# Early scores from straight q and k copies, and the experts' bias as a second matmul in the last half, in a two-layer attention and experts kernel

## The reference, cut to what matters

```python
# layer 1 (a = 0 in the kernel, work "p1" ahead of it, "p2" behind it)
x = x + attn(layernorm(x))        # q, k, v by one 8x24 matrix per head; softmax(att * mask), mask = tril(k=-1)
# layer 2 (a = 1, work "p2" ahead of it, "p3" behind it)
q_in = k_in = rope(xn); v_in = xn # causal softmax attention, xn = layernorm(x)
x1  = layernorm(xn + attn_out) * ln1_w + ln1_b
gates = softmax(x1 @ gate_w.T + gate_b); top_idx = top_k(gates, 2)
expert_outputs = einsum("bsd,efd->bsef", x1, expert_w) + expert_b     # 8 experts
moe = sum over the two chosen experts of expert_outputs * top_gates
out = x + layernorm(x1 + moe) * ln2_w + ln2_b
```

## Time and profile before

| | us |
|---|---|
| median of 3 runs | 789.04 (788.24 to 795.55) |
| the profiled execution's own time | 789.42 |
| its span in the trace | 787.6 |
| PE busy | 681.1 (86%) |
| ACT busy | 648.1 (82%) |
| DVE busy | 395.9 (50%) |
| POOL busy | 322.9 (41%) |

### The profile page before, as it was taken

How to read it: one execution, slowest core, us unless ns; L and a number is a source line. 1 busy time by engine, 2 the same in 40 slices (tenths; PEclk the granted TensorE clock), 3 DMA queues, 4 the chain that set the end, 5 groups by cost and what they waited for, 6 DMA issues and landing times. The chain is left out here.

```text
span 787.6 us, 15418 instructions
## 1 busy us (share of the span) xinstructions
PE 681.1 (86%) x5568; PEld 259.9 (33%) x5568; DVE 395.9 (50%) x1062; ACT 648.1 (82%) x721; POOL 322.9 (41%) x635
## 2 busy tenths in 40 slices
PE   4798998988899989989897989989999789999853
PEld 2333333433234333233232333233333233233422
DVE  5355344456445453556244644574345765455573
ACT  1499997999899997999698889998889798888721
POOL 3162235323633434434553245532666314424334
PEclk9589998999999997999898999999999999999976
DMA  6848357535567432424455244423545451230100
GB/s 162 288 136 263 101 202 239 178 127 202 181 213 243 162 110 86 148 83 135 143 163 155 104 141 130 146 83 121 190 151 179 158 162 60 70 96 1 41 13 15
DMA packets 77142, 109.86 MB, mean 139 GB/s; under 512 B 13928, under 2 KB 28400, under 8 KB 77040
## 3 DMA queue, kind: packets, MB, share of 16 engines
q1 hardware_dynamic: 72944, 107.32, 42.8%
q10 hardware_dynamic: 4096, 1.33, 0.8%
HBM read 60.94 MB, written 47.68 MB: 138 GB/s over the span
## 5 line engine op out<-in xcount | busy, mean ns | idle before, releaser
L1504 ACT ACTIVATE probs<-scores,shift 128x1024 f32<-128x1024 f32 x576 | 601.4, 1124 | 80.2 <-PE scores L1309 73.7
L1580 POOL TENSOR_SCALAR_AFFINE_SELECT probs<-probs 128x256 f32<-128x256 f32 (+1 forms) x448 | 197.5, 458 | 379.8 <-ACT probs L1504 379.1
L1334 PE MATMUL acc<-probs,v 128*9 128x512 f32 (+3 forms) x3072 | 322.2, 508 | 10.7 <-ACT num L1429 9.5
L1309 PE MATMUL scores<-qs,ks 32*128 32x512 f32 (+3 forms) x1536 | 185.1, 434 | 41.0 <-ACT probs L1504 37.4
L1309 PEld LDWEIGHTS scores<-qs,ks 32*128 32x128 f32 x1536 | 83.1, 189 | 259.9 <-ACT probs L1504 175.0
L1334 PEld LDWEIGHTS acc<-probs,v 128*9 128x9 f32 x3072 | 59.1, 100 | 132.2 <-issue 72.9
L1627 DVE TENSOR_TENSOR prod<-side,G 128x512 f32<-128x512 f32 x48 | 33.1, 691 | 89.3 <-PE side L1275 79.3
L1275 PE MATMUL side<-we,x1T 128*128 128x512 f32 x100 | 58.6, 669 | 0.8 <-DVE x1T L1916 0.8
L1561 POOL TENSOR_TENSOR moe<-psum 128x256 f32<-128x256 f32 x32 | 24.4, 762 | 51.3 <-DVE x1b L1627 26.6
L1429 ACT ACTIVATE num<-acc 128x512 f32<-128x512 f32 x64 | 38.2, 596 | 5.3 <-PE acc L1334 5.2
L1536 POOL TENSOR_TENSOR rstd<-rstd,expo 128x4 f32<-128x4 f32 x32 | 33.4, 1044 | 2.7
(11 more groups left out here) (186 smaller groups left out, 602.4 us busy)
## 6 DMA issues: line engine op xcount, KB each, us to landing
ks<-k_dram SPq DMA_DIRECT2D x96, 256.0 KB, 4.1
q_dram<-part SPq DMA_DIRECT2D x64, 256.0 KB, 3.5
qs<-q_dram SPq DMA_DIRECT2D x64, 256.0 KB, 3.2
num_dram<-num SPq DMA_DIRECT2D x60, 256.0 KB, 3.3
k_dram<-part SPq DMA_DIRECT2D x30, 256.0 KB, 4.0
xrow<-in_x SPq DMA_DIRECT2D x16, 256.0 KB, 4.4
nat<-num_dram SPq DMA_DIRECT2D x15, 256.0 KB
rdenb<-rden_dram SPq DMA_DIRECT2D x15, 256.0 KB
```

Source lines behind the costliest of these rows:

```text
L1309: ins = pe.matmul(dst, ks[u][r, kt // TH, (kt % TH) * P:(kt % TH + 1) * P], qs[u][r, q0:q0 + w], start=True, stop=not shifted)
L1334: ins = pe.matmul(acc[h * VW:h * VW + VC, q0:q0 + w], v9[V_OF[k]][:, kt, :, HG * hg + h], src, start=(s == 0), stop=last, skip_group_check ...
L1504: act.activation(dst, src, ACT.Exp, bias=shift[:, column(st):column(st) + 1], scale=SCALE).then_inc(probs_raw, 1)
L1580: ins = pool.affine_select(out=blocks, in_=blocks, compare_op=ALU.is_ge, fill=0.0, base=a - 1, pattern=[[0, blocks.shape[1]], [1, P]], cha ...
```

## The change

**At the start.** The first two passes (`STRAIGHT = 2`) no longer read q and k back from DRAM: six DMAs on SP's queue and two on ACT's copy 32 partitions of `part` straight into `qs` and `ks` as soon as `q` and `k` of the first half are read. The stores to DRAM stay (the second half's passes and the third pass on read them). DVE makes the rows of the first half ahead of `pairs`, and its q terms ahead of `roots`. Four of the jobs (`k` and `v` of the second half, both `suffix`) are issued by PE behind the scores of sets 0, 0, 1 and 3 (`BEHIND`), with banks given by hand (`BEFORE_BANKS`), and a set waits only for the jobs in its own banks (`PAIR_FREE`). The loads of `earlier8`, `bars8`, `cos` and `sin` move from ACT's queue to SP's, behind the stores of the second half. The planner's clocks of DVE and SP begin at 5.0, and it puts no jobs at the first sets, so 230 of its places (all in the first half of the stream) move by a few points.

**In the tail.** `GT` and `bias` of the last half are gone. Each of its eight `e0`/`e1` jobs gets a second matmul into the same bank, a row of ones by the row `be_row` of four experts' biases, and POOL adds `x1` itself. `stats`, `root`, `centre`, `scale` and `store` of that half become two sets, A for tiles 4 and 5, B for 6 and 7. The planner of `AFTER` has other rules: `num` first, and a read by ACT counts only once its operands are there.

```diff
+BEFORE_BANKS = {("p1", 0, "xT", 0): 1, ("p0", 0, "pairs", 0): 0, ("p0", 0, "bound", 0): 2, ("p1", 0, "q", 0): 3, ("p1", 0, "k", 0): 0,
+                ("p1", 0, "xT", 1): 4, ("p1", 0, "q", 1): 5, ("p1", 0, "k", 1): 4}
+BEHIND = {("p1", 0, "k", 1): 0, ("p1", 0, "v", 1): 0, ("p1", 0, "suffix", 1): 1, ("p1", 0, "suffix", 0): 3}
...
-    clock = {"PE": 0.0, "ACT": 0.0, "DVE": 0.0, "POOL": 0.0, "SP": 0.0}
+    clock = {"PE": 0.0, "ACT": 0.0, "DVE": 5.0, "POOL": 0.0, "SP": 5.0}
...
-        room = True
+        room = g > max(BEHIND.values())
...
+PAIR_FREE = [max(n for n in range(N_BEFORE) if JOB_BANK[n] // 2 == i) + 1 for i in range(PAIRS)]
...
+        def q_straight(engine, gp, i):
+            src = part[0][32 * gp:32 * gp + 32, 0, i, :].bitcast(F32)
+            engine.dma_start(qs[gp][i::2, :].bitcast(F32), src.unsqueeze(1).broadcast_to([32, 2, HALF])).then_inc(qs_in[gp], 16)
+        def k_straight(engine, gp, i):
+            engine.dma_start(ks[gp][i::2, 0, :].bitcast(F32), part[0][32 * gp:32 * gp + 32, 1, :, :].bitcast(F32)).then_inc(qs_in[gp], 16)
...
             for x in BEFORE:
+                if x[:4] == ("p1", 0, "parts_out", 0):
+                    sp.wait_ge(side_free, done(("p1", 0, "q", 0)))
+                    for i in range(2):
+                        q_straight(sp, 0, i)
+                    sp.wait_ge(side_free, done(("p1", 0, "k", 0)))
+                    k_straight(sp, 0, 0)
+                    for i in range(2):
+                        q_straight(sp, 1, i)
+                    k_straight(sp, 1, 0)
                 if x[5]:
                     turn(*x[:4])
                 if x[:4] == ("p1", 0, "parts_out", 0):
-                    load(0)
-                    load(1)
+                    load(2)
+            for t, d in ((earlier8, earlier8_d), (bars8, bars8_d)):
+                sp.dma_start(t[:, :], bc(d)).then_inc(late_weights_in, 16)
+            for t, d in ((cos, cos_d), (sin, sin_d)):
+                sp.dma_start(t[:, :, :], d.rearrange("(t p) f -> p t f", p=P)).then_inc(late_weights_in, 16)
...
-                if g == 0:
-                    pe.wait_ge(side_free, N_SCORES)
-                elif last >= PAIRS:
+                for unit in UNITS_OF[g]:
+                    if unit < PAIRS:
+                        pe.wait_ge(side_free, PAIR_FREE[unit])
+                if last >= PAIRS:
                     pe.wait_ge(probs_raw, last - PAIRS + 1)
...
                 if (work, b, name, i) == ("p1", 0, "parts_out", 0):
+                    act.wait_ge(side_free, done(("p1", 0, "k", 0)))
+                    for gp in range(STRAIGHT):
+                        k_straight(act, gp, 1)
                     k_out(act, 0, b, i)
...
-                        signal(pe.matmul(out[:, :], x1T[i // TH][:, i % TH, :], we[:, first:first + HALF], start=True, stop=True), last)
+                        alone = (1, b, i // TH) == LAST_HALF
+                        ins = pe.matmul(out[:, :], x1T[i // TH][:, i % TH, :], we[:, first:first + HALF], start=True, stop=not alone)
+                        if alone:
+                            ins = pe.matmul(out[:, :], ones[0:1, :], be_row[:, first:first + HALF], start=False, stop=True)
+                        signal(ins, last)
...
+        if alone:
+            for c, t in (("A", TH + 1), ("B", TH + 3)):
+                out[x("stats" + c)] = [("p3", b, "moe", t)]
+                out[x("root" + c)] = [x("stats" + c)]
+                out[x("centre" + c)] = [x("stats" + c)]
+                out[x("scale" + c)] = [x("centre" + c), x("root" + c), x("x2")]
+                out[x("store" + c)] = [x("scale" + c)]
```

More of the change, by code:

```diff
@@ L138 @@
               "root2": ("POOL", 1.3, 0.2), "centre2": ("DVE", 1.8, 0.1), "scale2": ("DVE", 1.6, 0.1), "store": ("SP", 0.5, 2.5)}
+for _c in "AB":
+    TURN_TIMES.update({f"stats{_c}": ("DVE", 0.8, 0.1), f"root{_c}": ("POOL", 1.3, 0.2), f"centre{_c}": ("DVE", 0.7, 0.1),
+                       f"scale{_c}": ("DVE", 0.7, 0.1), f"store{_c}": ("SP", 0.5, 2.5)})
 PIECES = {name: v[0] for name, v in JOB_TIMES.items()}
@@ L320, in p3 @@
         out[x("pick3")] = [x("pick2"), x("exp")]
-        out[x("GT")] = [x("pick3"), x("bias", 1)]
-        out[x("bias")] = [x("GT"), last("moe", 2)]
+        if not alone:
+            out[x("GT")] = [x("pick3"), x("bias", 1)]
+            out[x("bias")] = [x("GT"), last("moe", 2)]
         out[x("load2")] = [("p2", rows[0], "keep", rows[1])] + ([] if alone else [x("scale2", 1)])
@@ L325, in p3 @@
         for t in range(TH * j, TH * j + TH):
[L326 removed]
+            n = 2 if alone and t > TH else 1
+            out[("p3", b, "e0", t)] = [x("pick3"), ("p3", *((b, "e1", t - n) if t else (b - 1, "e1", T - 1)))]
             out[("p3", b, "e1", t)] = [("p3", b, "e0", t), ("p3", *((b, "moe", t - 2) if t >= 2 else (b - 1, "moe", T + t - 2)))]
[L328 removed]
+            out[("p3", b, "moe", t)] = [("p3", b, "e1", t)] + ([] if alone else [x("bias")])
+        if alone:
[5 more added lines that the diff above has]
+                out[x("store" + c)] = [x("scale" + c)]
+            ends[x("storeB")] = last_by(k, b, j) + 40
+            return
         out[x("stats2")] = [last("moe", 0)]
@@ L409, in operands @@
             before = [y for y in waits[x] if y[2] in ("e0", "e1")] + [(*x[0:2], "bias", (x[3] - 2) // TH)]
-            if any(y not in jobs for y in before):
+            if any(y not in jobs for y in before if y in waits or y in done):
                 return False
@@ L531, in left, with acts @@
         return way[x]
+    def acts(begun_job):
+        x, end = begun_job
+        needs = [y for y in waits[x] if y[2] in ("pick3", "e1", "GT")]
+        needs += [("p3", x[1], "pick3", x[3] // TH)] if x[2] in ("e0", "e1") else []
+        return max([clock["ACT"], end] + [done.get(y, 0.0) for y in needs]) + (1.2 if x[2] in ("e0", "e1") else 0.65)
     pending.sort(key=left, reverse=True)
@@ L538, in schedule @@
         if clock["PE"] <= t and (len(jobs) < first + 2 * PAIRS + 1 or banks[-1] <= t or len(begun) < 2 * PAIRS):
-            x = next((x for x in pending if x[2] in PIECES and operands(x, t)), None)
+            nums = any(y[2] == "num" for y in pending)
+            x = next((x for x in pending if x[2] in PIECES and (x[2] == "num" or not nums) and operands(x, t)), None)
             if x and len(begun) < 2 * PAIRS + 1:
@@ L547, in schedule @@
             x = next((x for x in pending if x[2] not in PIECES and turn_time(x)[0] == "DVE" and ready(x, t, NPOINT)), None)
-            if begun and begun[0][1] <= t and ready(begun[0][0], t, NPOINT) and (x is None or left(begun[0][0]) > left(x)):
-                x, _end = begun.pop(0)
+            act = acts(begun[0]) if begun and by_act(begun[0][0]) else t
+            if begun and begun[0][1] <= t and ready(begun[0][0], t, NPOINT) and (x is None or (left(begun[0][0]) > left(x) and act <= t + 0.3)):
+                x, end = begun.pop(0)
                 for c in range(PIECES[x[2]]):
@@ L553, in schedule @@
                 if by_act(x):
-                    clock["ACT"] = max(clock["ACT"], t) + (0.9 if x[2] in ("e0", "e1") else 0.6)
-                    t1, free, dve = clock["ACT"], 0.1, 0.75 if x[2] == "e1" else 0.1
+                    clock["ACT"] = acts((x, end))
+                    t1, free, dve = max(clock["ACT"], t), 0.1, 0.65 if x[2] == "e1" else 0.1
                 else:
@@ L577 @@
 BY_ACT = set(BY_ACT_ORDER)
-K_BY_ACT = [x[:4] for x in BEFORE if x[2] == "k" and x[5]]
+K_BY_ACT = [x[:4] for x in BEFORE if x[2] == "k" and x[5] and x[:4] not in BEHIND]
 TURNS = [x for x in BEFORE + sum(DURING, []) + AFTER if x[5]]
@@ L596 @@
 N_AFTER = sum(x[2] in PIECES and x[5] for x in AFTER)
-JOB_BANK = [n % (SPARE + 1) if n < N_BEFORE - 2 else SPARE for n in range(N_BEFORE)] + [SPARE] * (len(JOB) - N_BEFORE - N_AFTER)
+JOB_BANK = [BEFORE_BANKS.get(x, SPARE) for x in JOBS[:N_BEFORE]] + [SPARE] * (len(JOB) - N_BEFORE - N_AFTER)
 JOB_BANK += [n % (SPARE + 1) for n in range(N_AFTER)]
@@ L1371, in _, with behind @@
             for x in BEFORE:
-                turn(*x)
+                if x[:4] not in BEHIND:
+                    turn(*x)
             pe.wait_ge(narrowed, n_narrow)
+            def behind(g):
+                for x in BEFORE:
+                    if BEHIND.get(x[:4]) == g:
+                        turn(*x)
             def stretch(st, shifted):
@@ L1412, in _ @@
                     with pe.If(pe.value_load(flags[0:1, st:st + 1], min_val=0, max_val=1)):
+                        if st == 0:
+                            for g in range(SETS_ALL):
+                                behind(g)
                         exact(st)
@@ L1669, in project @@
                         dve.wait_ge(part_out[use % 2], stored(use - 2))
+                        if use == 2:
+                            for gp in range(STRAIGHT):
+                                dve.wait_ge(qs_in[gp], landed(gp))
                         if a0:
```

79 lines of the change are left out of this document (55 added, 24 removed), and 4 rows, old and new, of the table BEFORE_TURNS.

## The result

| | before | after |
|---|---|---|
| median, us | 790.88 (788.24 to 795.55, 4 runs) | 801.04 (800.15 to 803.55, 4 runs) |
| profiled execution, us | 789.42 | 803.55 |
| its span in the trace, us | 787.6 | 801.8 |

The account below looks back on a forecast made before the run. No engine was taken as busy throughout: ACT first with PE close behind in the stream, waiting chains at start and tail. 789.4 - 7.5 (start) - 3.4 (tail), stream 0, gave 778.5 us; forecast 776 to 781, range 774 to 785.5.

Parts of the forecast that it names:

- First exponential: Start: straight copies and later `suffix` let ACT's first exponential begin near 20.4 us, 10.7 us earlier.
- first two passes: Start: four more PE jobs between the sets cut the 10.7 us lead; 8.5 us earlier taken at their end.
- pass 3: Start: pass 3 is wanted at 39.5 and its late load costs 0 to 2 us, 1 taken.
- The copy's landing: Start: one straight copy from SBUF to SBUF takes 0.3 us for issue and 4.0 to land, pass 0 at 19.5.
- the port rule: Start: partitions 0 to 31 reach 8 of 16 ports; pass 0 would land 1.2 us later, time 779.7.
- The stream, "I put 0, with 1.5 either way": Attention stream: 230 plan steps move a few points, no work is added; cost 0, with 1.5 us either way.
- What is late next: Start: `load(3)` stands behind stores and four weight DMAs on SP's queue, issued at 32 to 36 us, landing 4 later.
- `num` first, `G` sooner: Tail: `num` ahead of `e0` brings `x1T` from 752.98 to 752.0; `G` comes at 760.9 in place of 764.3.
- So 32 passes ... one pass at 0.86 and 31 at 0.43: Tail: PE's 32 passes for the last half, nearly all at high clock, take 14.2 us and end at 773.8.
- rival 1: Tail: bias matmuls run at low clock; all 32 passes at 0.86 give 791.8 us, slower than before; chance 0.06.
- The tail: From behind the stream to the span's end: shorter by 3.4 us, at best 5.
- Against it: the clock rose in 760 to 765 while PE worked: Tail: argument against low clock in the bias matmuls, the granted clock having been 0.85 in that window before.

Follow-up runs that it names:

- Experiments 2: Kernel before with only the planner's new settings, so the new places of 230 steps, start and tail as before: 800.03 us, ratio 1.0128.
- 8: Changed kernel with early rows and 128-row bias, SP's planner clock at 2.0 in place of 0: 790.8 us, ratio 0.9983 to the kernel before.
- kernels 7: Changed kernel with old places, second batch's rows loaded early, four weight DMAs behind set 4, bias matmuls of 128 rows: 779.66 us, ratio 0.9854 to before.
- Experiment 9: Changed kernel with one step, POOL's `sq` in the third slot, two points later in the plan: 801.92 us, ratio 1.0129 to the kernel before.
- experiments 6: Changed kernel with old places, second batch's rows loaded early, four weight DMAs behind set 4, bias matmuls of 32 rows: 782.8 us, ratio 0.9883 to before.
- experiment 3: Changed kernel with the tail's bias matmul on 128 rows, 127 of them zero, in place of one: 796.62 us, ratio 1.0115 to the kernel before.
- 10: Old places, early rows, 128-row bias, plus DVE's second-batch stats and first rows moved earlier, POOL's root behind set 3: 775.88 us, ratio 0.9815 to before.

## Why the prediction was wrong

- **First exponential, first two passes, pass 3: right.** -10.1 for -10.7, -9.3 for -8.5 at the start of pass 2, and 1.97 us of wait ahead of pass 3 for "0 to 2". The copy's landing was the one term above its value (5.0 for 4.3). By the port rule of the Trainium skill ("SBUF — State Buffer", section "Door 1: The DMA port swizzle") pass 0 was to land at 20.7, and PE took its scores at 20.10, between the two forecasts. No run here varies the partitions, so the rule is neither borne out nor refuted.
- **The stream, "I put 0, with 1.5 either way": this step failed, by 14.7 us in this trace.** I took a plan's places for free because none adds work. Experiments 2 and 8 show what places are worth: 13.1 us from pass 4 to pass 20 in the kernel before, and one start value of the planner puts kernels 7 and 8 11 us apart. PE takes its side jobs in order, and five of them were 2.3 to 3.4 us late and held up scores. The orders of the two programs showed it: on POOL the root and `sq` changed places, and the transposes moved from point 14 to 20. Experiment 9 moved one of the steps back and won nothing, so which steps cost how much is open. Not every microsecond is traced: 7.1 us go between passes 4 and 16, where PE's waits of over 1 us at side jobs make 6.8 us, and 3.4 in before.
- **What is late next was only half asked.** I named `load(3)` behind SP's weight DMAs and priced it. The loads of the second batch's rows stand in the same queue, right behind it (37.28), and PE stood 2.89 us at their transposes; the rest of the 5.7 us between passes 3 and 4 came with PE's work at the low clock. DVE's 5 us at the flag were hidden here and came out only when the rows were early (experiments 6 and 7).
- **`num` first, `G` sooner: right.** Behind the last exponential, `x1T` came 0.9 us sooner (forecast 1.0) and `G` 2.7 sooner (3.4). The last `e1` was taken 10.2 us ahead of the span's end (10.3).
- **"So 32 passes ... one pass at 0.86 and 31 at 0.43": this step failed**, and rival 1 came true in kind, with a chance of 0.06 given. The first 8 of the 32 ran high and 24 took 1.00 us each: 24 x (1.00 - 0.43) = 13.7 us more, and experiment 3 gives back 61.9 - 48.0 = 13.9. The tail missed by less, 11.5 us (+8.1 for -3.4), as the clock had risen 21.0 us behind the last exponential (at 760.9) where 26.7 was forecast, and the work ahead of the 32 passes was sooner done. The rival's price, 0.86 a low pass, was itself too small: the change of shape comes on top. "Against it: the clock rose in 760 to 765 while PE worked" was no argument, as that work was all of 128 rows. With 128-row bias passes PE's last pass ends 37.7 to 39.8 us behind the last exponential (experiments 3 and 7), for 40.0 forecast, and the tail gains 3.8 to 5.8 for 3.4: the rest of the step's working holds.
- **The range.** It covered the start and put 1.5 us on a term whose size no row bounded. Both failed steps went the same way; only the early rise of the clock in the tail was luck. A table that moves 230 steps deserved the widest bound of all, and chances on both sides.

## What to carry to other kernels

When the head of a hand-planned schedule gets faster, every step behind it is due earlier, and the tables that fix its order must be made for the new times: look up, for each of the next jobs, when its data is loaded and what its engine does ahead of it. A plan that only "moves" is a change as large as any other and is measured by itself. And before small work is folded into TensorE's accumulation, count rows as well as columns: here the padding to 128 rows with zeros cost no time and saved 14 us over one row.

## What the runs showed of the hardware that was not expected

- With passes of one row between passes of 128 (two and two, 512 columns), PE busy throughout, the granted clock fell to 0.50 (1.2 GHz) and stayed there for 24 us. With 32 rows or 128 it stayed at 1.00 (2.4 GHz).
- Passes of 1 or 32 rows between passes of 128 start 0.53 us apart at the high clock, all of 128 rows 0.43; at the low clock 1.00 against 0.86.
- Behind DVE's reading of a flag and its jump over a branch stood a gap of 5.2 to 6.4 us in which it waited for nothing that the profile shows (experiments 7, 8 and 10), and one of 4.9 at a later slot.
- DVE's four `tensor_scalar` took 4.11 us beside 3.2 us of POOL's `tensor_tensor`, and 1.53 beside POOL's masks.
- One kernel under two names on one chip gave medians 0.7% apart (794.05 and 788.17).
